# The experts' down projection in three fp32r passes, one iteration later, with later weight requests

## The reference

```
x      = w_norm * rmsnorm(layernorm(X))
probs  = softmax(x @ w_router); w_topk, sel = top_k(probs, 4)       # 32 experts
buf    = rows of x that chose expert e, at most 128 of them         # [32, 128, 256]
g, u   = buf @ w_gate[e], buf @ w_up[e]                             # [128, 176] each
y      = (silu(g) * u) @ w_down[e]                                  # [128, 256]
out[token] += w_topk * y
out   += sigmoid(x @ w_shared_gate) * ((silu(x@sw_gate) * (x@sw_up)) @ sw_down)
result = X + 0.5 * (x + out)
```

## Time and profile before

| | |
|---|---|
| Median of the runs | 940.29 us (939.29 to 944.42) |
| The profiled execution | 938.85 us, of which its span is 937.0 us |
| Busy share of the span | TensorE 97%, VectorE 74%, ScalarE 57%, GpSimd 55% |
| TensorE in the chain that ended last | 63%; VectorE 18% |
| Experts' part of FFN1, first to last gate and up | 147.0 to 288.3 us |
| Experts' part of FFN2, first to last gate and up | 758.4 to 899.7 us |

### The profile page before, as it was taken

One profiled execution on the slowest core, in us unless ns is written; L12 is line 12 of the kernel. 1 busy time (PEld: TensorE's weight loads), 2 busy tenths in 40 slices (PEclk: granted clock), 3 DMA queues, 4 the chain that ended last, 5 costly groups with the idle time before them and its releaser, 6 DMA issues.

```text
span 937.0 us, 18000 instructions
## 1 busy us (share of the span) xinstructions
PE 909.6 (97%) x6118; PEld 685.6 (73%) x6118; DVE 695.9 (74%) x1704; ACT 531.3 (57%) x794; POOL 511.1 (55%) x537
## 2 busy tenths in 40 slices
PE   7999999999999999999999999989999999999997
PEld 6878887777778856666666666558788878777786
DVE  6998787555355889989998999988887875544435
ACT  6666743132233478878887888876667531322322
POOL 6343305565553588887888788934432055555530
PEclk9999999999999999999999999999999999999999
DMA  7143247777783610011001002004432377777735
GB/s 260 46 138 109 74 131 183 172 178 174 185 199 59 202 47 24 23 35 32 23 23 41 26 12 79 24 12 131 142 99 73 97 203 173 175 182 177 173 35 178
DMA packets 95512, 101.89 MB, mean 109 GB/s; under 512 B 18768, under 2 KB 86736, under 8 KB 95440
## 3 DMA queue, kind: packets, MB, share of 16 engines
q1 hardware_dynamic: 83152, 83.17, 29.5%
q0 software_dynamic: 12288, 17.83, 11.2%
HBM read 65.44 MB, written 35.54 MB: 108 GB/s over the span
## 4 chain that ended last, share of the span: by engine, by line
PE 63%; DVE 18%; issue 9%; ACT 4%; POOL 4%; DMA 1%; DVEq 0%; POOLq 0%; ACTq 0%
PE zT L1050 7%; PE gu L90 6%; PE gu L92 6%; PE gu L91 6%; PE gu L1070 6%; PE pj_at L90 3%; PE pv_at L1765 3%; PE pj_at L92 3%; PE pj_at L91 3%; PE down L90 3%; PE down L92 3%; PE down L91 3%; PE scores_at L1749 2%; PE zT L1059 2%; DVE turned_at L2007 2%
## 5 line engine op out<-in xcount | busy, mean ns | idle before, releaser
L90 PE MATMUL gu<-x_hi,gu_hi 128*128 128x512 f32 x264 | 120.4, 456 | 0.8 <-DVE act_gu L1353 0.7
L825 POOL DMA_INDIRECT rows<-z_rows,slots x64 | 69.3, 1083 | 67.9 <-DVE slots L1344 48.9
L1867 ACT ACTIVATE capped_at<-scores_at 128x2048 f32<-128x2048 f32 x64 | 93.1, 1454 | 20.5 <-PE scores_at L1749 20.3
L1130 ACT CAST a_hi<-act_gu 128x512 fp32r<-128x512 f32 x96 | 59.2, 617 | 79.1 <-DVE act_gu L1353 65.9
L92 PE MATMUL gu<-x_lo,gu_hi 128*128 128x512 f32 x264 | 103.9, 393 | 0.0
L91 PE MATMUL gu<-x_hi,gu_lo 128*128 128x512 f32 x264 | 103.6, 393 | 0.0
L1875 ACT ACTIVATE probs_at<-capped_at 128x2048 f32<-128x2048 f32 x64 | 95.1, 1487 | 2.5
L90 PE MATMUL down<-down_hi,a_hi 128*128 128x256 f32 x300 | 93.9, 313 | 0.6 <-DVE a_lo L1363 0.4
L1944 POOL TENSOR_SCALAR_AFFINE_SELECT probs_at<-probs_at 128x1024 f32<-128x1024 f32 x64 | 85.5, 1340 | 9.7 <-ACT probs_at L1875 9.0
L1050 PE MATMUL zT<-w_gu,xT 128*128 128x352 f32 x256 | 86.3, 460 | 0.0
L1232 ACT ACTIVATE y<-gu,rows 128x256 f32<-128x256 f32 x64 | 30.3, 473 | 98.5 <-PE gu L1070 89.0
(11 more groups left out here) (262 smaller groups left out, 2603.3 us busy)
## 6 DMA issues: line engine op xcount, KB each, us to landing
w_gu<-in_w_gate SPq DMA_DIRECT2D x64, 176.0 KB, 2.7
w_gu<-in_w_up SPq DMA_DIRECT2D x64, 176.0 KB, 3.3
w_down<-in_w_down SPq DMA_DIRECT2D x64, 176.0 KB
z_rows<-z SPq DMA_DIRECT2D x16, 512.0 KB, 3.6
acc<-base SPq DMA_DIRECT2D x10, 512.0 KB, 3.4
out<-base SPq DMA_DIRECT2D x10, 512.0 KB, 3.3
xn_at<-acc SPq DMA_DIRECT2D x16, 256.0 KB, 2.8
x<-xn_at SPq DMA_DIRECT2D x16, 256.0 KB, 2.1
```

The costliest lines, as they stand in the source:

```text
L90: nc.tensor.matmul(out, w_hi, x_hi, start=first, stop=False)
L825: pool.indirect_dma_start(out=gathered_rows[:, n, :], out_offset=None, in_=m.z_rows, in_offset=bass.IndirectOffsetOnAxis(ap=slots[:, e:e + ...
L1867: nc.scalar.activation(capped[:, u % 2, :, 0:n], scores[:, :, 0:n], ACT.Tanh, scale=QK_SCALE / SOFTCAP).then_inc(capped_ready, 1)
```

## The change

The down projection of an expert gets the same split as the shared expert's: the products and `w_down` are each split into a high part (fp32r, by ScalarE) and a low part (the rest, by VectorE), and six fp32r matmuls of 256 columns take the place of the four recorded fp32 ones. The down projection of e moves behind gate and up of e+1 (the last one behind the first piece after the experts); the products are transposed into the upper half of the PSUM bank whose lower half holds `y`, so that they wait for `scale` of the expert before. The loads of weights wait for GpSimd too: gate and up of e behind `add` of e-4 and the gather behind it, `w_down` of e-1 right after them. `w_down` has three buffers instead of four, `y` lies in a buffer of `base` that is free by then. Cut to what acts in the loops:

```diff
-            for e in range(HELD_W):
-                if e == EARLY - 1:
-                    reached(sp, gathered[1], 16)
-                if e >= EARLY:
-                    load_gate_up(e)
-                load_down(e)
+            load_down(0)
+            load_down(1)
+            reached(sp, gathered[1], 16)
+            load_down(2)
+            load_gate_up(EARLY)
             for e in range(HELD_W, E):
+                reached(sp, weights_due, e - HELD_W + 1)
                 reached(sp, gu_done, e - HELD_W + 1)
                 load_gate_up(e)
-                reached(sp, y_ready, e - HELD_W + 1)
-                load_down(e)
+                load_down(e - 1)
+            reached(sp, weights_due, E - HELD_D)
+            load_down(E - 1)
...
                 add(e)
                 if e + HELD_ROWS < E:
                     gather(e + HELD_ROWS)
+                pool.sem_inc(weights_due, 1)
...
             def turn_products(e):
                 reached(pe, prod_done, e + 1)
-                reached(pe, xT_copied, min(e + 2, E))
+                if e == 0:
+                    reached(pe, lists_ready, 2)
+                at_least(pe, y_scaled, e)
                 for k in range(2):
                     last = nc.tensor.transpose(prodT_ps[:, k, :], prod[:, e % 2, k:FE:2], m.ident[:])
                 last.then_inc(prodT_ready, 1)
+            def down_expert(e):
+                n = e % 2
+                reached(pe, w_down_lo_made, e + 1)
+                reached(pe, prodT_lo_ready, e + 1)
                 for k in range(2):
-                    last = nc.tensor.matmul(y_ps, prodT[:, e % 2, k, :], w_down[:, n, k, :], start=k == 0, stop=k == 1)
+                    last = split_matmul(nc, y_ps, prodT_hi[:, k, :], prodT_lo[:, k, :], w_down_hi[:, n, k, :],
+                                        w_down_lo[:, n, k, :], k == 0, k == 1)
                 last.then_inc(y_ready, 1)
...
             for e in range(E):                                   # TensorE
+                if e == 1:
+                    down_expert(0)
+                gate_up_expert(e)
                 if e + 1 < E:
                     turn_rows(e + 1)
-                gate_up_expert(e)
-                *earlier_pieces, last_piece = pieces_beside(e)
-                for p in earlier_pieces:
+                if e > 1:
+                    down_expert(e - 1)
+                first_piece, *later_pieces = pieces_beside(e)
+                piece(first_piece)
+                turn_products(e)
+                for p in later_pieces:
                     piece(p)
-                turn_products(e)
-                piece(last_piece)
                 if e < 12 and e % 2 == 0:
                     find(2 + e // 2)
-                down_expert(e)
             for p in range(behind_experts, LAST_PIECE):
                 piece(p)
+                if p == behind_experts:
+                    down_expert(E - 1)
...
+            def high_products(e):                                # ScalarE
+                reached(act, prodT_ready, e + 1)
+                at_least(act, y_ready, e)
+                nc.scalar.copy(prodT_hi[:], prodT_ps).then_inc(prodT_hi_ready, 1)
+            def high_down(e):
+                reached(act, w_down_loaded[e % HELD_D], 16 * (e // HELD_D + 1))
+                at_least(act, y_ready, e - 1)
+                nc.scalar.copy(w_down_hi[:, e % 2], w_down[:, e % HELD_D]).then_inc(w_down_hi_made, 1)
...
             for e in range(E):                                   # ScalarE
+                if e == 1:
+                    scale(0)
                 silu_expert(e)
-                for p in pieces_beside(e):
+                if e > 1:
+                    scale(e - 1)
+                first_piece, *later_pieces = pieces_beside(e)
+                followup(first_piece)
+                high_products(e)
+                high_down(e)
+                for p in later_pieces:
                     followup(p)
-                scale(e)
...
+            def low_products(e):                                 # VectorE
+                reached(dve, prodT_hi_ready, e + 1)
+                dve.tensor_tensor(prodT_lo[:], prodT_ps, prodT_hi[:].bitcast(F32), ALU.subtract).then_inc(prodT_lo_ready, 1)
+            def low_down(e):
+                reached(dve, w_down_hi_made, e + 1)
+                dve.tensor_tensor(w_down_lo[:, e % 2], w_down[:, e % HELD_D], w_down_hi[:, e % 2].bitcast(F32), ALU.subtract
+                                  ).then_inc(w_down_lo_made, 1)
...
             for e in range(E):                                   # VectorE
+                lists = e < 12 and e % 2 == 1
+                product_expert(e)
                 if e + 1 < E:
                     copy_rows(e + 1)
-                first, *middle, last_piece = pieces_beside(e)
-                followup(first)
-                product_expert(e)
-                for p in middle:
+                if lists:
+                    list_places(2 + e // 2)
+                first_piece, *later_pieces = pieces_beside(e)
+                followup(first_piece)
+                low_products(e)
+                if lists:
+                    list_tokens(2 + e // 2)
+                low_down(e)
+                for p in later_pieces:
                     followup(p)
-                copy_products(e)
-                followup(last_piece)
-                if e < 12 and e % 2 == 0:
-                    list_experts(2 + e // 2)
```

More of the change, by code:

```diff
@@ L50 @@
 HELD_W = 4
+HELD_D = 3
 HELD_ROWS = 6
@@ L475, in ffn @@
         in_tile = sb("in_tile", [P, E8, P], BF16)
-        to_end = sb("to_end", [P, E8, P], BF16)
         below = sb("below", [P, 2, 4, P - 1], BF16)
-        xT = sb("xT", [P, 2, KC, CAP], F32)
+        with ExitStack() as until_listed:
+            to_end = sb("to_end", [P, E8, P], BF16, until_listed)
         silu_e = sb("silu_e", [P, 2, FE], F32)
         prod = sb("prod", [P, 2, FE], F32)
-        prodT = sb("prodT", [FD, 2, 2, CAP], F32)
-        y = sb("y", [P, HELD_Y, C], F32)
-        w_down = sb("w_down", [FD, HELD_W, 2, C], F32)
+        xT = sb("xT", [P, 2, KC, CAP], F32)
+        prodT_hi = sb("prodT_hi", [FD, 2, CAP], F32R)
+        prodT_lo = sb("prodT_lo", [FD, 2, CAP], F32R)
+        w_down = sb("w_down", [FD, HELD_D, 2, C], F32)
+        w_down_hi = sb("w_down_hi", [FD, 2, 2, C], F32R)
+        w_down_lo = sb("w_down_lo", [FD, 2, 2, C], F32R)
         if attention_next:
@@ L518, in ffn @@
         x_lo = [x_lo[:, n] for n in range(HELD_X - 1)] + [x_lo_third[:], x_lo_fourth[:]]
+        y = base[:, HELD_X - 1]
         base = [base[:, n] for n in range(HELD_X)] + [base_fourth[:]]
@@ L569, in ffn @@
         w_gu_loaded = [sem(f"w_gu_loaded{n}", 32 * (E // HELD_W)) for n in range(HELD_W)]
-        w_down_loaded = [sem(f"w_down_loaded{n}", 16 * (E // HELD_W)) for n in range(HELD_W)]
+        w_down_loaded = [sem(f"w_down_loaded{n}", 16 * len(range(n, E, HELD_D))) for n in range(HELD_D)]
+        w_down_hi_made = sem("w_down_hi_made", E)
+        w_down_lo_made = sem("w_down_lo_made", E)
         gathered = [sem(f"gathered{n}", 16 * len(range(n, E, HELD_ROWS))) for n in range(HELD_ROWS)]
@@ L577, in ffn @@
         prodT_ready = sem("prodT_ready", E)
-        prodT_copied = sem("prodT_copied", E)
+        prodT_hi_ready = sem("prodT_hi_ready", E)
+        prodT_lo_ready = sem("prodT_lo_ready", E)
         y_ready = sem("y_ready", E)
@@ L581, in ffn @@
         added = sem("added", 16 * E)
+        weights_due = sem("weights_due", E)
         def block_rows(dram, b):
@@ L738, in load_down @@
             def load_down(e):
-                sp.dma_start(w_down[:, e % HELD_W, :, :], ins["w_down"][e].rearrange("(p k) n -> p k n", k=2)
-                             ).then_inc(w_down_loaded[e % HELD_W], 16)
+                at_least(sp, w_down_lo_made, e - HELD_D + 1)
+                sp.dma_start(w_down[:, e % HELD_D, :, :], ins["w_down"][e].rearrange("(p k) n -> p k n", k=2)
+                             ).then_inc(w_down_loaded[e % HELD_D], 16)
             def slot(b, f, r, s):
@@ L1038, in turn_rows @@
                 at_least(pe, xT_copied, e)
-                at_least(pe, prodT_copied, e - 1)
                 for k in range(KC):
@@ L1227, in silu_expert @@
                 nc.scalar.activation(silu_e[:, e % 2, :], gu_ps[:, 0, :], ACT.Silu).then_inc(silu_done, 1)
+            def high_products(e):
[6 more added lines that the diff above has]
+                nc.scalar.copy(w_down_hi[:, e % 2], w_down[:, e % HELD_D]).then_inc(w_down_hi_made, 1)
             def scale(e):
+                if e == 0:
+                    reached(act, base_stored, 16 * (NB - MERGED))
                 reached(act, y_ready, e + 1)
@@ L1251, in on_scalar @@
             for e in range(E):
+                if e == 1:
+                    scale(0)
                 silu_expert(e)
-                for p in pieces_beside(e):
+                if e > 1:
[5 more added lines that the diff above has]
```

(12 more changed lines are left out.)

12 lines of the change are left out of this document (1 added, 11 removed).

## The result

The changed kernel takes 999.31 us (median of 4 runs, 997.37 to 1005.04) against 941.0 for the kernel before, run beside it: a ratio of 1.064 [1.061, 1.067]. The forecast was 937.4, the range 920 to 951. The profiled execution took 998.92, with a span of 997.1 and a mean granted clock of 0.993 against 0.999 before. That difference is worth some 6 of the 60 us at most (an estimate, 0.006 of the span), so the clock is not the main cause.

The account below looks back on a forecast made before the run. TensorE was taken to bound the experts, DMA second. A stage: -13.7 saving, +10.9 new waits, +2.0 requests = -0.8; two stages -1.6, boundary -1.3, so 940.29 - 2.9 = 937.4 us, range 920 to 951.

Parts of the forecast that it names:

- Weight requests: Experts' loads: requests leave 3.0 us after an add's start, add interval 4.3, costing 2.0 us a stage (-1 to 14).
- the 6.17: GpSimd's adds before the change: one interval of 6.17 us with gate weights asked 0.23 ahead, against 4.22 asked 0.77 ahead.
- the adds become the bound: Rival, experts: weight bursts meet each next add's rows, TensorE takes GpSimd's pace; 950 us (945 to 957), chance 0.23.
- Six matmuls in 0.70: Down projection on TensorE: six fp32r matmuls take 0.70 us instead of 0.96, saving 8.3 for 32 experts of a stage.
- The transposes wait for the scale: Product's transposes on TensorE wait for the previous expert's scale beside one piece: 0 to 0.2 us, 0.05 taken, 1.6 together.
- the wait of 0.34: Experts with two pieces: transposes wait 0.34 us for VectorE's product; it goes, 16 times, saving 5.4 us a stage.
- First expert: Start of a stage: down projection precedes the second gate, so TensorE waits for low `w_down`; 2.1 us (0 to 2.75).
- the other five late experts: Later waits for VectorE's results: shared product on a first piece 1.8 us, three block ends 3.3, plus list rounds.
- the lists: Six list rounds on VectorE between product and low `w_down` in three-piece experts: 0.35 us each, 2.1 together.
- Ideal saving: Experts on TensorE: cheaper passes (8.3) and the vanished product wait (5.4) save 13.7 us a stage before new waits.
- End of FFN1: Boundary to attention: adds end closer behind TensorE, so its 1.30 us wait at attention's statistics goes.

Follow-up runs that it names:

- e3: The kernel before with only the wait of gate and up requests for the GpSimd sequencer's mark behind add and gather, old passes kept: 996.0 us, ratio 1.060.
- e6: The changed kernel with later experts' weight loads cut to one partition, so requests stay but bytes go and weights are stale: 940.2 us, one run.
- e1_mark: The changed kernel with the mark set by a GpSimd memset behind add and gather instead of a sequencer increment: 944.61 us, ratio 1.0066 to the kernel before.
- e5: The kernel before with gate and up requests held to a GpSimd memset between add and gather, old passes kept: 938.71 us, ratio 0.9991.
- e1b: The changed kernel with the mark set by a GpSimd memset between add and gather: 942.84 us, ratio 1.0035 to the kernel before.

## Why the prediction was wrong

**The step that failed** is *Weight requests*: "Now gate, up and `w_down` go out 832.44 + 1.09 - 830.54 = 3.0 after the add's start, so some 1.4 ahead of the next one". They go out 0.3 after it. The sum took the end of the gather's descriptors for the moment of the mark, because the mark's line stands behind it. No row of before shows a semaphore set behind an indirect DMA, and the step should have had two ends: 0.3, the gap to the next instruction, and 3.0. The cost taken was 2.0 a stage (-1 to 14); measured by e3 alone, 28.3 and 23.7, and by the changed kernel against e6, some 28 and 27.

The step also read its rows too narrowly. It has SyncE ask "at any point of an add" and sets the 6.17 against a gate asked 0.23 ahead; but in 33 of the 64 adds of that trace the gate was asked between 0.5 ahead and 0.14 after the start, and they landed in a median of 4.3. The add with the 6.17 is the longest of them, at 5.9. Those rows priced two loads at an add's start, and cheaply; no row priced three in one burst.

The Trainium skill (Perfetto Trace Analysis, section DMA Instruction — SWDGE (GPSIMD)) says that GpSimd's sequencer is ready for its next instruction once it has pushed such a DMA, while other processors write the descriptors. The trace agrees, with 0.3 us from the add's start to SyncE's request, where the add's descriptors take 1.59.

The rule of turns between queues that the prediction weighed (the Trainium skill, DMA: Bandwidth & Descriptors, section Queues, rings and completion order) gave "up to that row's 2 us" for loads that run while the rows move. The trace agrees: the median landing is 5.5, which is 1.6 above the 3.9 of e6, where no bytes stand beside the rows. What was unforeseen is the place of the burst.

**The rival named for it**, "the adds become the bound", was right in mechanism, "the burst meets each next add's rows, and TensorE [...] takes on GpSimd's pace", save that the burst meets the same add's rows and not the next one's. Its price of 950 rested on 4.67 an interval; 5.73 and 5.59 came.

**The other steps**, read from e6 and e1_mark, in which the requests do no harm or stand where the prediction had them:

- *Six matmuls in 0.70*: right. In e6, weight loads in order of time, one down projection, a piece and the product's transposes; the second fence is ScalarE in the same stretch:
```profile
875.38 0.19 PEld L91 LDWEIGHTS gu<-w_down_hi,prodT_hi 88*128 88x128 f32 x1
...
876.08 0.19 PEld L91 LDWEIGHTS gu<-x_hi,gu_hi 128*128 128x128 f32 x1
...
876.99 0.24 PEld L1074 LDWEIGHTS gu<-ident,prod 128*88 128x88 f32 x2 [0.36 <-issue]
```
```profile
876.40 0.47 ACT L1262 ACTIVATE base<-gu,rows 128x256 f32<-128x256 f32 x1 [0.81 <-PE gu L93]
```
- *The transposes wait for the scale* was taken at 0.05 an expert (0 to 0.2). The piece should be followed at 876.78; it is at 876.99, 0.12 after the scale's end at 876.87. So 0.21. Of the 19 such waits of the stretch 18 end 0.11 to 0.12 after a scale's end; at 0.21 each that is some 4.0 (an estimate from this one) in place of 1.6. The profile files this wait under "issue". For the same reason the wait of 0.34 did not wholly go: an expert with two pieces takes 3.92, not 3.71.
- *First expert* 6.20 between gates against 4.75, so 1.45 later (2.1 taken); the other five late experts cost 3.8 (1.8 + 3.3 + part of the lists taken). Right in kind and near in size.
- *Ideal saving* of 13.7 a stage: too high. An expert with two pieces saved 4.31 - 3.92 = 0.39 in place of 0.60, for 16 of them 3.4 less (the scale is the cause of most of it), and one with three pieces, mostly 4.48 to 4.60, saved 0.08 to 0.20 in place of 0.26. Net of all waits a stage lost 0 to 1.4 where 2.8 were to be gained. The 1.4 is FFN1's: behind the first expert's wait of 1.96 us TensorE's granted clock stands at 0.50, the lower of its two levels, for 3.4 us from 152.9, and the second expert takes 5.24 there, 3.70 in FFN2, where the same wait was followed by no such stretch.
- *End of FFN1*: the 1.30 did not wholly go. TensorE waits 1.1 for VectorE at attention's statistics in the changed kernel, where the adds end last again, 0.8 in e6 and 0.5 in e1_mark.

e1_mark is the kernel that the prediction thought it had before it: requests 3.1 after an add, landings of 4.0. By its ratio it is 6.2 us slower than the kernel before, where 2.9 faster was forecast: the rest of the sum was 9 us too kind, and the requests account for the other 55.

## What to carry to other kernels

On GpSimd, an increment of a semaphore that stood behind an indirect DMA in the program came 0.3 us after that DMA's start, with 1.59 us of descriptors still to make: it marked neither the DMA's work nor its descriptors. Read such a moment off the trace, or let an instruction that the engine executes set the mark. Ask of every burst which transfer with a wait on its landing it will meet, and how long the burst is; here 528 KB requested 0.3 us after an add's start cost 57 us (e3 against e5), at 1.7 us nothing, and 352 KB 0.1 us after it next to nothing. And before work is spread over idle engines, ask which part of it needs no fresh result, and put that part ahead of the part that does: that order was the difference between no gain and 4.5 us a stage.

## What the runs showed of the hardware

- An increment by GpSimd's own queue, behind an add and a gather whose descriptors take 1.59 and 1.05 us, released SyncE 0.3 us after the add's start (changed kernel, e3); a memset in the same place released it 3.1 us after (e1_mark).
- A memset right behind an add starts 1.08 us after it and ends after the add's descriptors; the gather starts 1.89 after the add with the memset between them and 1.90 without. GpSimd in e1b:
```profile
190.72 1.59 POOL L845 DMA_INDIRECT acc<-base,slots  x1 [1.52 <-DMA acc<-base,slots]
191.80 0.62 POOL L885 MEMSET mark<- 128x1 f32 x1
192.61 1.05 POOL L837 DMA_INDIRECT rows<-z_rows,slots  x1 [0.19 <-issue]
```
- The rows of an add, 128 of 1 KB, move in 1.5 us nearly alone (e1b), and in 3 us beside three loads of 176 KB (changed kernel).
